# An adaLN transformer pair on one Trainium2 core: batch 1's expert rows summed inside layer 1's attention

## The reference, cut to what matters

```python
h = _layernorm(x, axis=-1) * (1 + cb) + sb
x = x + gb * _L0_ffn_ref(h, ...)          # out = sum over a token's 8 experts + sh_g * sh_out
...
h = _layernorm(x, axis=-1) * (1 + ca) + sa
x = x + ga * _L1_attn_ref(h, ...)
# in _L1_attn_ref
q, k, v = x @ W_query, x @ W_key, x @ W_value      # split into 16 heads
scores = jnp.einsum('bhqd,bhkd->bhqk', q, k)       # causal mask, then softmax
ctx = jnp.einsum('bhqk,bhkd->bhqd', attn, v)
```

## Time and profile before

| | before |
|---|---|
| median of 3 runs | 1199.86 us (1199.67 to 1203.19) |
| profiled execution | 1203.47 us, span of its trace 1201.7 us |
| busy, share of the span | PE 75%, PEld 48%, DVE 72%, ACT 47%, POOL 43% |
| gathers of the expert sum | 128, from 462.4 to 630.1 us |
| attention's block | from 639.5 us |
| maxima | 256, from 665.7 to 892.3 us |
| last score tile starts | 932.6 us |

### The profile page before, as it was taken

How to read it: one execution, slowest core, us unless ns; L and a number is a source line. 1 busy time by engine, 2 the same in 40 slices (tenths; PEclk the granted TensorE clock), 3 DMA queues, 4 the chain that set the end, 5 groups by cost and what they waited for, 6 DMA issues and landing times. The chain is left out here.

```text
span 1201.7 us, 16894 instructions
## 1 busy us (share of the span) xinstructions
PE 907.1 (75%) x5172; PEld 581.4 (48%) x5172; DVE 869.8 (72%) x2535; ACT 567.8 (47%) x1243; POOL 520.3 (43%) x532
## 2 busy tenths in 40 slices
PE   6899976888888884000007989999988899999887
PEld 5766744666666663000004433333322467688565
DVE  6467887599989873566445888878887569777465
ACT  3322267566666662000004366777768543434553
POOL 3100048777777764777774431111112144453000
PEclk9989985899999997555557999999999999999899
DMA  5060161677767765333332622222211300110001
GB/s 160 1 278 19 38 158 26 187 212 209 211 205 211 220 206 180 103 98 97 103 94 87 214 84 72 72 72 72 72 19 27 118 27 28 52 53 1 1 27 45
DMA packets 74522, 124.97 MB, mean 104 GB/s; under 512 B 12282, under 2 KB 52288, under 8 KB 73024
## 3 DMA queue, kind: packets, MB, share of 16 engines
q1 hardware_dynamic: 58944, 81.80, 22.3%
q0 software_dynamic: 15360, 41.96, 12.5%
q10 hardware_dynamic: 128, 0.13, 0.1%
HBM read 83.80 MB, written 35.66 MB: 99 GB/s over the span
## 5 line engine op out<-in xcount | busy, mean ns | idle before, releaser
L2026 DVE CUSTOM_DVE_ANT_0 masked<-ps,causal 128x128 f32<-128x128 f32 (+7 forms) x256 | 181.1, 755 | 40.7 <-PE ps L1825 39.7
L1539 POOL DMA_INDIRECT h_t<-modulated_rows,ga_rows x192 | 182.8, 952 | 60.8 <-issue 55.2
L145 PE MATMUL ps<-consts,xn 128*128 128x128 f32 x128 | 20.1, 308 | 177.1 <-PEq L78 104.2
L1551 POOL DMA_INDIRECT big<-expert_rows,slot x128 | 126.0, 984 | 55.2 <-issue 40.5
L2006 ACT ACTIVATE xn<-ps 128x512 f32<-128x512 f32 (+3 forms) x256 | 111.7, 511 | 43.6 <-PE ps L1847 42.7
L1458 DVE SCALAR_TENSOR_TENSOR xn<-big,weights,xn 128x256 f32<-128x256 f32 x128 | 62.5, 488 | 84.4 <-DMA big<-expert_rows,slot 80.4
L151 ACT ACTIVATE h_t<-ps,modc 128x512 f32<-128x512 f32 x24 | 17.4, 778 | 192.3 <-PE ps L145 97.9
L1130 PE MATMUL ps<-h_t,xn 128*128 128x128 f32 x768 | 104.9, 281 | 0.0
L145 PEld LDWEIGHTS ps<-consts,xn 128*128 128x128 f32 x128 | 16.8, 160 | 182.0 <-issue 109.9
L1130 PEld LDWEIGHTS ps<-h_t,xn 128*128 128x128 f32 x768 | 96.5, 197 | 0.9 <-issue 0.9
L1118 PE MATMUL ps<-consts,h_t 128*128 128x128 f32 x384 | 64.5, 292 | 35.9 <-DMA h_t<-modulated_rows,ga_rows 35.5
(11 more groups left out here) (321 smaller groups left out, 2184.4 us busy)
## 6 DMA issues: line engine op xcount, KB each, us to landing
expert_rows<-h_t SPq DMA_DIRECT2D x96, 256.0 KB, 2.6
qk<-qk_parts SPq DMA_DIRECT2D x72, 128.0 KB, 2.7
big<-in_gu SPq DMA_DIRECT2D x8, 1024.0 KB, 11.2
qk_parts<-parts SPq DMA_DIRECT2D x16, 384.0 KB, 2.6
raw<-in_mlp SPq DMA_DIRECT2D x16, 384.0 KB, 3.1
room<-in_down SPq DMA_DIRECT2D x4, 1024.0 KB, 10.7
h_t<-modulated_rows,ga_rows POOLq DMA_INDIRECT x192
h_t<-qk_parts SPq DMA_DIRECT2D x24, 128.0 KB, 2.7
```

The lines of the kernel that those rows point to most:

```text
L1539: nc.gpsimd.indirect_dma_start(xg[:, u % 4, i, :], None, row_dram, bass.IndirectOffsetOnAxis(ap=idxg[:, 2 * u + i:2 * u + i + 1].bitcast(U ...
L1551: nc.gpsimd.indirect_dma_start(yg[:, t % 2, k, :], None, y_dram, bass.IndirectOffsetOnAxis(ap=slots[:, n:n + 1].bitcast(U32), axis=0))\
L2026: nc.vector.tensor_tensor_reduce(masked[:, at % 2, 0:k], ps[:, bank:bank + (k + GW - 1) // GW, :] .rearrange("p a n -> p (a n)")[:, 0:k], ...
```

## The change

The expert sum's stage now handles tiles 0 to 7 alone. For tiles 8 to 15 it only adds the shared expert's row (`shared_add`). Weights, row numbers and the gate row of batch 1 are copied to a place that lives on (`late`). The 64 gathers of batch 1 (`fetch`) are issued by GpSimd in the attention's block: 16 among the parts of batch 0's products, 16 behind them, and 32 behind masks of rounds 0 and 1 (`FETCHED`). They land in the half of the values' tile `vs` that batch 1's values take later. VectorE sums tiles 8 and 9 before the first maximum and tiles 10 to 15 behind the maxima that `SUMMED` names, in the place of `wo`, whose load moves to round 4.

Batch 1's turned rows, products and values are no longer interleaved with round 0. They are 16 late items in `entries`, behind maxima 2 to 9 and 14 to 21 of round 3, each with one bank of the maxima's ring. VectorE alone takes them out of PSUM (`late_out`); for a product it writes part 1 and the remainder, and GpSimd parts 2 and 3 (`late_parts`) behind a mask (`PARTED`: products 8 and 9 behind step 8 of round 1, 10 and 11 behind step 9, 12 behind step 0 of round 2, 13 to 15 behind step 1). SP stores these eight parts just before the load of round 4. The diff, dedented:

```diff
+late = swap[:, 3 * KC * D:3 * KC * D + 2 * TB * TOPK + D]
+late_weight = late[:, 0:TB * TOPK].rearrange("p (t k) -> p t k", t=TB)
+late_slot = late[:, TB * TOPK:2 * TB * TOPK].bitcast(I32)
+late_gate = late[:, 2 * TB * TOPK:]
...
+def shared_add(t):
+    link(nc.vector.tensor_tensor(xn[:, t, :], xn[:, t, :], rows_b[:, 2, t // TB, :], ALU.mult))
+    link(nc.vector.tensor_tensor(x_tok[:, t, :], x_tok[:, t, :], xn[:, t, :], ALU.add))
+nc.vector.tensor_copy(late_weight.rearrange("p t k -> p (t k)"),
+                      w8[:, TB:, :].rearrange("p t k -> p (t k)"))
+nc.vector.tensor_copy(late_slot, slots[:, TB * TOPK:])
+link(nc.vector.tensor_copy(late_gate, rows_b[:, 2, 1, :]))
 dve.wait_ge(s_she, NT)
-for t in range(NT):
+for t in range(TB):
+    shared_add(TB + t)
     combine(t)
     if 1 <= t < 7:
         conditioned(t - 1)
-    if t in (7, 8):
-        guarded(t - 7)
-    if t in (3, 7):
+    if t == 6:
+        guarded(0)
+        guarded(1)
+    if t == 3:
         dve.wait_ge(s_ac, t + 1)
-        ln_stats(t // 4, link)
-    if t in (5, 9):
-        ln_rows(dve, (t - 5) // 4, s_early, 2)
-dve.wait_ge(s_ac, NT)
+        ln_stats(0, link)
+    if t == 5:
+        ln_rows(dve, 0, s_early, 2)
+dve.wait_ge(s_ac, TB)
+ln_stats(1, link)
+ln_rows(dve, 1, s_early, 2)
+dve.wait_ge(s_early, GB)
...
-for t in range(NT):
+for t in range(TB):
     if t >= 2:
         pool.wait_ge(s_ac, t - 1)
     for k in range(TOPK):
...
             yg[:, t % 2, k, :], None, y_dram,
             bass.IndirectOffsetOnAxis(ap=slots[:, n:n + 1].bitcast(U32), axis=0))\
             .then_inc(s_yg[t % 2], 16)
-    if t in (5, 9):
-        ln_pool(pool, 2, ((t - 5) // 4,))
+    if t == 5:
+        ln_pool(pool, 2, (0,))
+ln_pool(pool, 2, (1,))
...
+late_h = sb(vst, "late_h", [P, KC, GW])
+late_rows = sb(vst, "late_rows", [P, 4, D])
+late_rest = late_rows[:, :, :].rearrange("p (r a) d -> p r (a d)", a=2)
...
-NJ = 4 * NG
+s_back = [sem(f"e_back{n}") for n in range(2)]
+s_sum, s_late_p1, s_late_p2 = [sem(f"e_{n}") for n in ("sum", "late_p1", "late_p2")]
+NJ = 4 * GB
+back = vs[:, HEADS:].rearrange("p u t n -> p (u t n)").rearrange("p (s k d) -> p s k d", s=2, k=TOPK)
...
+LATE_V, FIRST_LATE = NV // BATCH - 1, (2, 14)
+late_items = [[("turned", GB + g, c) for c in range(KC)]
+              + [("product", j, None) for j in range(NJ + 4 * g, NJ + 4 * g + 4)]
+              + [("value", p, None) for p in range(2 * g, 2 * g + 2)] for g in range(GB)]
 entries = []
 for v in range(NV + 1):
     for n in range(HQ * TB):
         if v < NV:
             entries.append((v, n))
+            if v == LATE_V:
+                entries.extend((v, late_items[g][n - FIRST_LATE[g]]) for g in range(GB)
+                               if 0 <= n - FIRST_LATE[g] < len(late_items[g]))
...
+FETCHED = {(0, 0): 2, (0, 1): 2, (0, 2): 2, (0, 3): 6, (0, 8): 2, (0, 9): 2, (0, 10): 2, (0, 11): 2,
+           (1, 0): 2, (1, 1): 2, (1, 2): 2, (1, 3): 6}
+LATE_POW = ((0, 3), (1, 10))
+SUMMED = {(1, 6): 10, (1, 12): 11, (1, 20): 12, (2, 5): 13, (2, 18): 14, (2, 24): 15}
+LATE_STATS = {(1, 14): GB, (2, 25): GB + 1}
+LATE_ROWS_AT = {(1, 24): GB, (3, 12): GB + 1}
+PARTED = {}
+for j in range(NJ, 2 * NJ):
+    index = place[LATE_V, ("product", j, None)]
+    at = next(n for n, d in enumerate(due) if d > index) // HQ
+    PARTED.setdefault(divmod(next(n for n in range(at, NV * NTI) if n % NTI in diagonal), NTI),
+                      []).append(j)
...
+def store_parts(j):
+    g, w, m = projected(j) if j < NJ else late_projected(j)
+    b, col = g // GB, (g % GB) * GW
+    sp.wait_ge(s_p3, j + 1)
+    sp.dma_start(qk_dram[w, :, b * D + m * P:b * D + (m + 1) * P, col:col + GW]
+                 .rearrange("n p c -> p n c"), parts[:, j % 4]).then_inc(s_sts[j % 4], 16)
...
-if v and v + 2 < NV:
-    if v + 2 == NV // BATCH:
-        for i in range(4):
-            sp.wait_ge(s_sts[i], 16 * NG)
+if v and v + 2 < NV and v + 2 != NV // BATCH:
+    sp.wait_ge(s_st, v * STEPS)
+    load_qk(sp, v + 2)
+if v + 2 == NV // BATCH:
+    for j in range(NJ, 2 * NJ):
+        store_parts(j)
+    for i in range(4):
+        sp.wait_ge(s_sts[i], 16 * NG)
     sp.wait_ge(s_st, v * STEPS)
     load_qk(sp, v + 2)
 if v:
     store(v - 1)
+if v == NV // BATCH:
+    sp.wait_ge(s_sum, TB)
+    sp.dma_start(wo[:, :, :], a["wo1"].rearrange("(k p) n -> p k n", p=P)).then_inc(s_wo, 16)
+    sp.dma_start(bo[:, :], a["bo1"]).then_inc(s_wo, 16)
...
+fetched = [0]
+def fetch(count):
+    for n in range(fetched[0], fetched[0] + count):
+        t, k = divmod(n, TOPK)
+        if k == 0 and t >= 2:
+            pool.wait_ge(s_sum, t - 1)
+        nc.gpsimd.indirect_dma_start(
+            back[:, t % 2, k, :], None, y_dram,
+            bass.IndirectOffsetOnAxis(ap=late_slot[:, n:n + 1].bitcast(U32), axis=0))\
+            .then_inc(s_back[t % 2], 16)
+    fetched[0] += count
+def late_parts(j):
+    pool.wait_ge(s_mx, place[LATE_V, ("product", j, None)] + 1)
+    nc.gpsimd.tensor_copy(part2[:, j % 4, :], late_rest[:, j % 2, :]).then_inc(s_late_p2, 1)
+    pool.wait_ge(s_late_p2, j - NJ + 1)
+    nc.gpsimd.tensor_tensor(part3[:, j % 4, :], late_rest[:, j % 2, :], part2[:, j % 4, :],
+                            ALU.subtract).then_inc(s_p3, 1)
...
+fetch(5)
 for j in range(NJ):
     pool.wait_ge(s_p2, j + 1)
     if j >= 4:
         pool.wait_ge(s_sts[j % 4], 16 * (j // 4))
     nc.gpsimd.tensor_tensor(part3[:, j % 4, :], rest[:, j % 4, :], part2[:, j % 4, :],
                             ALU.subtract).then_inc(s_p3, 1)
-    if j == 7:
-        nc.gpsimd.memset(vs[:, :, :, HD:], 1.0).then_inc(s_ones, 1)
-    if j == 11:
-        pool.wait_ge(s_p3, j + 1)
-        nc.gpsimd.memset(ks[0][KR:KM, :, :], 1.0).then_inc(s_ones, 1)
-        pool.wait_ge(s_ones, 2)
-pool.wait_ge(s_vp, NT // 2)
+    fetch(1)
+fetch(3)
+nc.gpsimd.memset(vs[:, 0:HEADS, :, HD:], 1.0).then_inc(s_ones, 1)
+pool.wait_ge(s_p3, NJ)
+pool.wait_ge(s_ones, 1)
+nc.gpsimd.memset(ks[0][KR:KM, :, :], 1.0).then_inc(s_ones, 1)
+pool.wait_ge(s_ones, 2)
+pool.wait_ge(s_vp, TB // 2)
 pool.wait_ge(s_proj, NJ)
-pool.wait_ge(s_p3, NJ)
+fetch(2 * TOPK)
...
+if (v, n) in FETCHED:
+    fetch(FETCHED[v, n])
+if (v, n) == LATE_POW[0]:
+    ln_pool(pool, 2, (GB,))
+if (v, n) == LATE_POW[1]:
+    ln_pool(pool, 2, (GB + 1,))
+if (v, n) == (1, 11):
+    pool.wait_ge(s_sum, TB)
+    nc.gpsimd.memset(vs[:, HEADS:, :, HD:], 1.0).then_inc(s_ones, 1)
+for j in PARTED.get((v, n), ()):
+    late_parts(j)
...
+def late_item(bank, kind, which, c):
+    if kind == "turned":
+        pe.wait_ge(s_ln, which - GB + 1)
+        for i in range(4):
+            last = nc.tensor.transpose(ps[:, bank, i * P:(i + 1) * P],
+                                       late_rows[:, i, c * P:(c + 1) * P], ident)
+    elif kind == "product":
+        g, w, m = late_projected(which)
+        pe.wait_ge(s_mx, place[LATE_V, ("turned", g, KC - 1)] + 1)
+        for k in range(KC):
+            last = nc.tensor.matmul(ps[:, bank, :], wqkv1[:, w, k, m * P:(m + 1) * P],
+                                    late_h[:, k, :], start=k == 0, stop=k == KC - 1)
     else:
-        valued(TB + u - 16, 0 if u % 2 else u // 2 + 5)
-for g in range(GB):
-    transposed(g + 1)
-    for j in range(4 * g, 4 * g + 4):
-        for k in range(KC):
-            product(j, k)
-transposed(NG - 1)
+        for t in range(TB + 2 * which, TB + 2 * which + 2):
+            for k in range(KC):
+                last = nc.tensor.matmul(ps[:, bank, (t % 2) * D:(t % 2 + 1) * D],
+                                        late_h[:, k, t % 4 * P:(t % 4 + 1) * P],
+                                        wqkv1[:, 2, k, :], start=k == 0, stop=k == KC - 1)
+    last.then_inc(s_si, 1)
...
+def summed(t):
+    n = t - TB
+    row = wo[:, n % 2, :]
+    dve.wait_ge(s_back[n % 2], 16 * TOPK * (n // 2 + 1))
+    e_link(nc.vector.tensor_scalar(row, back[:, n % 2, 0, :], late_weight[:, n, 0:1], None,
+                                   ALU.mult))
+    for k in range(1, TOPK):
+        e_link(nc.vector.scalar_tensor_tensor(row, back[:, n % 2, k, :],
+                                              late_weight[:, n, k:k + 1], row,
+                                              ALU.mult, ALU.add))
+    e_link(nc.vector.tensor_tensor(row, row, late_gate, ALU.mult))
+    nc.vector.tensor_tensor(x_tok[:, t, :], x_tok[:, t, :], row, ALU.add).then_inc(s_sum, 1)
+def normed_late(g):
+    dve.wait_ge(s_rstd, 2 * NG + g + 1)
+    if g > GB:
+        dve.wait_ge(s_p3, NJ + 4)
+    for t in range(4 * g, 4 * g + 4):
+        last = nc.vector.tensor_scalar(late_rows[:, t % 4, :], x_tok[:, t, :], mv[:, t, 0:1],
+                                       rstd[:, t:t + 1], ALU.subtract, ALU.mult)
+    last.then_inc(s_ln, 1)
+def late_out(bank, kind, which, c):
+    if kind == "turned":
+        return nc.vector.tensor_scalar(late_h[:, c, :], ps[:, bank, :], mod_col(1, SCALE_A, c, which // GB),
```

(25 more changed lines are left out.)

85 lines of the change are left out of this document (28 added, 57 removed).

## The result

| | before | after |
|---|---|---|
| median (4 runs each) | 1199.76 us | 1250.47 us |
| ratio, 95% interval | | 1.0416 (1.0389 to 1.0443) |
| span of the profiled execution | 1201.7 us | 1249.5 us |
| last tile of the block summed | 637.9 | 550.15 |
| attention's first instruction | 639.56 | 560.53 |

The change costs 50.7 us. The forecast was 1202, with a range to 1218: wrong. Counted along the path, span against span (47.9 us), stretch by stretch, growth and in brackets the forecast: up to the attention's first instruction -79.0 (-80.7); from there to the first score tile +10.5 (+3.8); to (3,0) +71.4 (+56.9); to (4,0) +35.7 (+22.1); to the last score tile +3.0 (0); from there to the end +6.2 (0). No single step failed alone; every stretch behind the sum stage came out dearer.

What follows compares the result with a forecast made beforehand. No single engine was taken to bound the whole: gather issue bound the expert sum, TensorE and VectorE the attention. -80.7 + 3.8 + 56.9 + 22.1 = +2.1 us gave 1202 against the median; own range 1193 to 1211, wider 1180 to 1218.

Steps and rivals of the forecast that it cites:

- 1, the stage that is halved: Expert sum up to the attention's first instruction: 86.9 us become 6.2 behind tile 7, with a block exit of 1.64; -80.7 us.
- 2, to the first score tile: Attention's start to first score tile: first maximum 10.1 us later behind tile 9's sum, then 27.0 instead of 33.3; +3.8 us.
- 3, to (3,0): First score tile to round 3's first maximum: VectorE work 34.3 plus gather waits 25.6, less 3 absorbed; +56.9 us.
- 8 us were free, of these I count 3: VectorE between first score tile and round 3: 8 us of its time were free, 3 of them would absorb added work.
- 4, (3,0) to (4,0): First maximum of round 3 to that of round 4: late items 28.5, then an uncovered chain 22.5, for 28.9 before; +22.1 us.
- The chain behind product 15: Product 15 to round 4's first maximum: mask, GpSimd's parts, store, twelve loads and landing, covered by nothing; 22.5 us.
- Eight products of two matmuls 8.0: TensorE among round 3's maxima: the eight late products take two matmuls each, 8.0 us in all.
- 10 us idle ahead of (4,0): TensorE ahead of round 4's first maximum: an idle stretch of some 10 us that ends with a load.
- 5, behind (4,0): Rounds 4 to 7 and after: unchanged, with wo's later load and the half fill of ones at no cost; 0.
- B: Rival for the attention's gathers: in time, with 8 of the 25.6 us of waits left; 1184, chance 0.25.
- C: Rival for the attention's gathers: sharing DMA engines, three sets land after 7.1 us, not 2.8; +13, 1215, chance 0.17.
- D: Rival, the SBUF port: eight GpSimd masks each stop a VectorE sum in the attention, at most 5.1 us; 1207, chance 0.08.

Runs made afterwards that it cites:

- the late norms: Changed kernel with all 16 tiles gathered and summed in the experts' block, so only batch 1's norm, turned rows, products and values stand in the attention: 1.0299.
- the short sums: Changed kernel with one gather a token tile for batch 1 and the seven multiply-adds of each of its sums left out: 0.9777.
- the whole ones: Changed kernel with one gather a token tile instead of eight for batch 1, the sum adding the same row eight times: 1.0006.
- The run that lowered the clock by 0.04 alone: Kernel with only the late items moved, plus 24 unused VectorE multiplies ahead of the first maximum: 1.0368 against 1.0299 without them.
- the filled ones: Five kernels with repeated or unused TensorE matmuls, three on the changed kernel (1.0639, 1.0517, 1.0823), two on that with one gather a tile (1.0493, 1.0216).
- later sums: Changed kernel with the sums of tiles 12 to 15 behind later maxima and group 3's statistics behind maximum 1 of round 3: 1.0226.
- the first filling: Changed kernel with repeated bf16 matmuls of maxima, 32 of them ahead of maximum 4 but behind a wait for VectorE: 1.0639.

## Why the prediction was wrong

**1, the stage that is halved** (-80.7, was -79.0). Gathers and sums were right: tile 7 was done 2.5 us before the forecast point. The failing term is the block's exit, read as 1.64: that was what showed behind VectorE's last sums, not what GpSimd needs. Behind GpSimd's power it was 5.8. A longer border came again, unforecast, at the attention's end (5.12 for 0.96), the larger part of the tail's +6.2. Most of the rest there is TensorE's first matmuls, at a granted clock of 0.50 behind that wait (9.54 us for 7.10).

**2, to the first score tile** (+3.8, was +10.5). The order was right, VectorE at tile 9's sum ahead of all maxima. The last gather started 30.1 us after the block's start (28.6 forecast) and landed after 5.7, not 2.8, while the DMA engines moved 370 GB/s; with tile 9's sum the first maximum was at 41.2 (36.2). From there to the first score tile it took 28.8, not 27.0. Tile 8's multiply-adds, beside GpSimd's third parts, took 6.32 and undisturbed ones 3.61, at no cost here, since VectorE then waited 6.4 for tile 9. The windows ahead of the landings of tiles 9 and 14 (last number: GB/s):

```profile
590.00:596.30 6.30, 1.23 (x4) 0.40 (x4) 0.00 (x0) 0.00 (x0) 5.88 (x4) 0.51 1.06 370
...
708.00:717.10 9.10, 1.42 (x15) 0.56 (x13) 0.53 (x4) 2.25 (x7) 4.61 (x6) 0.77 0.82 199
```

**3, to (3,0)** (+56.9, was +71.4). Two runs split it: 29.3 for the waits (25.6 forecast), 24.5 for the multiply-adds (21.7 of work), 17.6 for what is left of the sums, the statistics and rows, which are 12.6 of work, and for the 1.5 of wait in that run. The step that failed is "8 us were free, of these I count 3": nothing was free. VectorE's work, 34.3 counted, cost 42.1. Its idle time other than for gathers rose with the work, from 6.5 us before to 8.5 with the late norms, 11.0 with the short sums and 15.8 with the whole ones, while TensorE's mean clock went 1.00, 0.94, 0.77, 0.70. What grew is VectorE's wait for scores (5.6, 7.0, 9.4, 12.6); the first and the last of these:

```profile
DVE masked L2026 <- PE ps L1825: 5.6, 12, 0.8
...
DVE masked L2102 <- PE ps L1909: 12.6, 14, 2.1
```

So VectorE, once back from a sum, waits longer for TensorE than before. Two causes fit: TensorE at the lower clock, and TensorE stopped at full banks during the sum and behind afterwards at either clock. The run that lowered the clock by 0.04 alone lost 1.2 us, the filled ones could not separate the two, and so the clock's share stays open. The Trainium skill (TensorE: Matmul & The Clock Gate, HAM oscillation) says that waits between bursts of matmuls let the clock fall again and again; the trace agrees, 0.63 from 630.5 to 752.9 with TensorE busy for 66 of 122 us, against 1.00 at 45.7 of 51.0 before. I had taken TensorE's durations at full clock and never asked what VectorE's stops would do to them.

**4, (3,0) to (4,0)** (+22.1, was +35.7). The chain behind product 15 came out near: from its last matmul at 796.55 to (4,0) 20.9 us (22.5), of which GpSimd's three pairs of parts took 5.4 and not 7.3. The mis-sized term is the work ahead of it, 28.5 forecast and 43.7 measured. "Eight products of two matmuls 8.0" read 16 matmuls of the trace as eight products when they were four; a product takes 1.93 and not 1.0. Likewise a value item takes 2.25 and not 1.0, since it is two value tiles. Counted rightly, TensorE has 16.8 + 15.4 + 2.9 + 4.5 = 39.6 us there, and the part comes out at +33. (VectorE's terms add up to 28.2, not 28.4, which changes nothing.) That TensorE binds the work up to product 15 held; the "10 us idle ahead of (4,0)" did not appear: TensorE was kept so long behind product 15, by its own work and by what that waited for, that the load came only 1.5 us late:

```profile
794.67 1.88 PE L1991 MATMUL ps<-late_h,swap 128*128 128x512 f32 x4
...
817.08 0.22 PE L1907 MATMUL ps<-qk 96*128 96x128 bf16 x1 [1.49 <-DMA qk<-qk_parts]
```

**5, behind (4,0)** (0, was +3.0 to the last score tile). Half of it is the first round behind (4,0), 30.4 us for 28.9; no run was made to find its cause.

**Rivals.** B (gathers in time) was false as built; made true by order or by fewer gathers it gave 19 to 29 us of the path's time. C (landings over 4 us) was true for one of the four sets of part 3: tile 14's last gather, issued in a stretch of 199 GB/s, landed after 4.5 us, 1.7 more than the 2.8 of tiles 12, 13 and 15.

```profile
712.59 0.94 POOL L1826 DMA_INDIRECT v_ones<-expert_rows,swap  x1 [0.30 <-issue]
...
717.11 0.35 DVE L2137 TENSOR_SCALAR wo<-v_ones,swap 128x256 f32<-128x256 f32 x1 [8.58 <-DMA v_ones<-expert_rows,swap]
```

The rest of the 28.1 us is the gathers' place behind masks; later sums left 0.5 us of all these waits. D (the port): the eight sets of seven multiply-adds took 32.3 us from first to last, against 28.9 at the undisturbed 3.61. Of these 3.4 us 2.7 are tile 8's, beside GpSimd's subtractions, and 0.7 those of tiles 10 and 11, where one mask each fell into an add; in part 3 that is 0.7 us where 5.1 had been the price, since the masks hardly met the sums. The length of one multiply-add (ns: least, median, most):

```profile
L2140 DVE SCALAR_TENSOR_TENSOR wo<-v_ones,swap,wo x56: 483/485/1884, 582.7 to 741.5; 128x256 f32<-128x256 f32 x56
```

The Trainium skill's rule (SBUF — State Buffer, Who interferes with whom) shows in tile 8's sum, where two adds took 1.88 and 1.76 us beside subtractions of 1.16; a mask of 0.64 made an add 0.3 to 0.4 us longer.

**What bounds the gain.** An estimate for each tile: moved out of the gather-bound stage it saves 10 us. In the attention it costs 4.85 or more for its sum, in series, 4.6 for its share of the late items (37.2 over eight), and its gather waits. With every gather wait and seven of eight gathers gone the change only breaks even (1.0006), because the attention had no engine with time to spare where the work went.

## What to carry to other kernels

Work moved into a stage where two engines are at about 90% cost more than its duration here, 42.1 us for 34.3, whatever the slack in the average; count such work at 1.0 or above unless the trace shows whose idle time takes it. When an engine stops for it, ask what the others then wait for. Count matmuls in the trace against the program's loops before pricing one of them. And a stage's end that looks cheap may be cheap only because another engine's last work covers it. Before comparing runs from two chips, compare a stretch that no edit touched.

## What the runs showed of the hardware that was not expected

- A block's end was longer with many gathers in it: TensorE's wait at the attention's end was 5.12 us with 64 gathers, 0.96 with 8 or none. At the first border 7.2 us passed from GpSimd's last instruction to the next block. What GpSimd does in that time, no run shows.
- Five fillings of TensorE gave a mean granted clock of 0.66 to 0.92 from the first score tile to (3,0); unfilled it was 0.63, and 0.70 with one gather. TensorE was busy for 67% of that stretch both in the kernel with one gather (0.70) and in the first filling (0.82), so the busy share of a stretch does not tell its clock.
- A two-input multiply-add of VectorE took 0.49 us alone and 0.48 to 0.55 beside gathers, 1.88 and 1.76 beside a subtraction of GpSimd of 1.16, and 0.85 and 0.79 beside a mask of 0.64.
- The last gathers of tiles 12, 13 and 15 landed after 2.8 us, and those of tiles 14 and 9 after 4.5 and 5.7, while the DMA engines moved 199 and 370 GB/s.
- On some chips TensorE is idle with nothing in the profile that it waits for: 52.8 us on one line of the experts' stage, and 16.1 us among the first 32 maxima while gathers were being issued, with the same program. Why, no run shows.
